# Query split of a cross-attention search: fetching the first tile's columns in the stage and the other seven tiles' during the first tile's search

## The reference

```python
Q = (x_text @ Wq).reshape(Bb, Tt, H, DH)
K = (x_vision @ Wk).reshape(Bb, Gg, H, DH)
scores = jnp.einsum('bthd,bghd->bhtg', Q, K) / np.sqrt(DH).astype(np.float32)
scores = jnp.where(vision_mask[:, None, None, :], scores, -jnp.inf)
topv, topi = jax.lax.top_k(scores, K_TOP)        # K_TOP = 32
probs = jax.nn.softmax(topv, axis=-1)
attn = jnp.zeros_like(scores).at[bi, hi, ti, topi].set(probs)
attn_mean = attn.mean(axis=1)
c_t = jnp.einsum('btg,bgd->btd', attn_mean, x_vision @ Wv) * text_mask[..., None]
```

## Time and profile before

| what | value |
|---|---|
| median of 3 executions | 1713.12 us (1707.66 to 1718.37) |
| the profiled execution, its own time | 1714.1 us |
| its span | 1712.2 us |
| mean granted TensorE clock | 0.921 of full speed |
| busy: TensorE, VectorE, ScalarE, GpSimd | 82%, 75%, 55%, 41% of the span |
| bytes moved by DMA | 37.34 MB |

### The profile page before, as it was taken

The page is one execution under the profiler, slowest core; times in us unless marked ns, Lnnn a source line. Parts: engine busy times, 40 slices in busy tenths (PEclk is TensorE's granted clock), DMA queues, the critical chain, the costliest instruction groups (busy, mean ns, idle before and its releaser), DMA issues. The chain is left out here.

```text
span 1712.2 us, 20081 instructions
## 1 busy us (share of the span) xinstructions
PE 1399.5 (82%) x6652; PEld 718.6 (42%) x6653; DVE 1280.9 (75%) x3087; ACT 943.4 (55%) x1500; POOL 706.9 (41%) x545
## 2 busy tenths in 40 slices
PE   5777799999987657889888898988957539999798
PEld 2223344333334512455454444544645423333365
DVE  4999667855515669999999999999948566766433
ACT  4665211566623302888888888888821236666321
POOL 2664212022002000989998898989810030000012
PEclk9899899999997967999999999999978658999899
DMA  6000111000009420000000000000030120000000
GB/s 148 1 1 0 33 56 42 0 1 0 0 5 201 86 63 1 1 1 1 1 1 1 1 1 1 1 1 1 1 96 9 34 64 1 1 1 1 1 1 13
DMA packets 29962, 37.34 MB, mean 22 GB/s; under 512 B 12975, under 2 KB 23087, under 8 KB 28723
## 3 DMA queue, kind: packets, MB, share of 16 engines
q1 hardware_dynamic: 27294, 22.31, 4.8%
q10 hardware_dynamic: 2552, 13.63, 3.9%
HBM read 29.68 MB, written 6.24 MB: 21 GB/s over the span
## 5 line engine op out<-in xcount | busy, mean ns | idle before, releaser
L1557 PE MATMUL psum<-film_ka,film_context_qa 97*128 97x512 bf16 (+1 forms) x832 | 323.7, 390 | 89.3 <-DVE search_and_weigh_e L1791 38.1
L1758 DVE MAX8 search_and_weigh_kept<-psum 128x8 f32<-128x171 f32 (+2 forms) x1216 | 331.5, 327 | 14.4 <-PE psum L1559 14.1
L1559 PE MATMUL psum<-film_kb,film_context_qb 128*128 128x512 bf16 (+1 forms) x832 | 320.3, 386 | 0.0
L1944 ACT ACTIVATE search_and_weigh_e<-psum,search_and_weigh_bias 128x512 f32<-128x512 f32 (+1 forms) x416 | 268.1, 666 | 60.6 <-PE psum L1559 58.7
L1791 DVE SCALAR_TENSOR_TENSOR search_and_weigh_e<-psum,film_context_top,search_and_weigh_e 128x512 f32<-128x512 f32 (+1 forms) x283 | 200.6, 716 | 14.2 <-ACT search_and_weigh_e L1944 12.4
L1814 POOL TENSOR_TENSOR search_and_weigh_e<-search_and_weigh_e,search_and_weigh_keep 128x512 f32<-128x512 f32 (+1 forms) x133 | 150.6, 1132 | 100.1 <-ACT search_and_weigh_keep L1923 96.8
L1557 PEld LDWEIGHTS psum<-film_ka,film_context_qa 97*128 97x128 bf16 x832 | 86.0, 103 | 237.9 <-DVE search_and_weigh_e L1791 103.3
L3057 POOL TENSOR_TENSOR residual<-residual,top_expert_kept 128x1024 f32<-128x1024 f32 x7 | 16.4, 2348 | 295.4 <-DVE top_expert_kept L3014 295.4
L1818 POOL TENSOR_TENSOR search_and_weigh_mean<-search_and_weigh_e 128x512 f32<-128x512 f32 (+1 forms) x104 | 133.5, 1284 | 11.5 <-DVE search_and_weigh_e L1791 4.3
L1848 PEld LDWEIGHTS psum<-ctx_rows,search_and_weigh_mean_T 128*128 128x128 f32 (+1 forms) x816 | 122.6, 193 | 30.4 <-issue 4.1
L1823 POOL TENSOR_TENSOR search_and_weigh_mean<-search_and_weigh_mean,search_and_weigh_e 128x512 f32<-128x512 f32 (+1 forms) x104 | 128.0, 1230 | 8.2
(11 more groups left out here) (549 smaller groups left out, 2642.6 us busy)
## 6 DMA issues: line engine op xcount, KB each, us to landing
film_kb<-film_k_rows ACTq DMA_DIRECT2D x4, 1601.0 KB
film_ka<-film_k_rows ACTq DMA_DIRECT2D x3, 1601.0 KB
ctx_T<-in_ctx_T SPq DMA_DIRECT2D x1, 2401.5 KB
gqa_experts_w<-in_L_ffn_W SPq DMA_DIRECT2D x1, 2048.0 KB
film_convolve_back<-in_dft_back SPq DMA_DIRECT2D x1, 1728.0 KB, 13.3
film_k_rows<-cross_attention_film_hi SPq DMA_DIRECT2D x6, 256.0 KB, 2.1
film_k_rows<-cross_attention_film_mid SPq DMA_DIRECT2D x6, 256.0 KB, 2.0
film_k_rows<-cross_attention_film_low SPq DMA_DIRECT2D x6, 256.0 KB, 2.0
```

Of the source, the lines that this page charges most:

```text
L1557: pe.matmul(out, a["qa"][0:ROWS, h, rows], a["ka"][0:ROWS, h, c + b:c + b + cols], start=True, stop=False)
L1559: last = pe.matmul(out, a["qb"][:, h, rows], a["kb"][:, h, c + b:c + b + cols], start=False, stop=True)
L1758: last = dve.max(kept[:, h % 2, first + s, :], bank[:, lo:hi])
L1944: act.activation(e[:, n % RING, sub, 0:PIECES[u][1]], ps[:, SEARCH_BANKS + q % WEIGH_BANKS, 0:PIECES[u][1]], ACT.Exp, bias=bias[:, i % 2, ...
```

## The change

The DRAM tensor `q_rows` and a new semaphore `other_tiles` are made in `film_context`, so that both blocks can use them. The helper `fetch_queries` issues the fetches of one part for a given range of columns. In `split_queries`, ScalarE's seven fetches now bring columns 0 to 127 only, that is the first of the eight tiles: 32 KB each instead of 256 KB, still in 128 pieces. SyncE still waits for seven landings. In `search_and_weigh`, SyncE begins with seven fetches of columns 128 to 1023 (224 KB each), ahead of its loads of `mask8` and `w_v`. TensorE waits for `other_tiles` before piece r = 52, the first piece of tile 1. What is computed stays the same.

```diff
--- before.py
+++ after.py
@@ -1453,10 +1453,23 @@
          "eighth": m.sb("eighth", [P, NT * NH]),
          "mask8": m.sb("mask8", [P, NT], U8), "mask": m.sb("mask", [P, NT]), "w_v": m.sb("w_v", [DC, D]),
 
-         "count": m.sb("count", [1, NT * NH + 1], mybir.dt.int32)}
+         "count": m.sb("count", [1, NT * NH + 1], mybir.dt.int32),
+         "q_rows": nc.dram_tensor("q_rows", (3, P, S), BF16).ap(), "other_tiles": m.sem("other_tiles")}
     for part in (split_queries, search_and_weigh, search_general, weigh_again):
         with ExitStack() as ctx:
             part(nc, g, t, Memory(nc, ctx, part.__name__), a)
+
+
+
+QUERY_PLACES = ((("qa", 0), ("qb", 0), ("qb", 2)), (("qa", 1), ("qb", 1), ("qb", 3)), (("qa", 2),))
+N_FETCHES = 7
+
+
+def fetch_queries(eng, a, k, cols, done):
+
+    for name, r in QUERY_PLACES[k]:
+        eng.dma_start(a[name][r * DH:(r + 1) * DH, :, cols],
+                      a["q_rows"][k].rearrange("(h d) s -> d h s", d=DH)[:, :, cols]).then_inc(done, 16)
 
 
 def split_queries(nc, g, t, m, a):
@@ -1473,7 +1486,7 @@
     rest = m.sb("rest", [P, S])
     parts = m.sb("parts", [P, 3, S], BF16)
     hi, mid, low = (parts[:, k, :] for k in range(3))
-    q_rows = nc.dram_tensor("q_rows", (3, P, S), BF16).ap()
+    q_rows = a["q_rows"]
 
     loaded, ones_set, chain_dve = m.sem("loaded"), m.sem("ones_set"), m.sem("chain_dve")
     var_ready, root_ready, xn_ready, xT_psum, xT_ready, q_done, q_ready = (
@@ -1493,7 +1506,7 @@
             sp.dma_start(w_q[:], t["L1_xattn_Wq"]).then_inc(loaded, 16)
             for k in range(3):
                 store(k)
-            sp.wait_ge(spread, 16 * 7)
+            sp.wait_ge(spread, 16 * N_FETCHES)
 
         @block.vector
         def _(dve):
@@ -1530,15 +1543,9 @@
                 act.activation(q[:, n * HALF:(n + 1) * HALF], ps[:, 2 + n, :], ACT.Copy,
                                scale=float(DH) ** -0.5).then_inc(q_ready, 1)
 
-            def fetch(k, places):
+            for k in range(3):
                 act.wait_ge(stored[k], 16)
-                for dst, r in places:
-                    act.dma_start(dst[r * DH:(r + 1) * DH, :, :],
-                                  q_rows[k].rearrange("(h d) s -> d h s", d=DH)).then_inc(spread, 16)
-
-            fetch(0, ((qa, 0), (qb, 0), (qb, 2)))
-            fetch(1, ((qa, 1), (qb, 1), (qb, 3)))
-            fetch(2, ((qa, 2),))
+                fetch_queries(act, a, k, slice(0, P), spread)
 
         @block.gpsimd
         def _(pool):
@@ -1854,6 +1861,8 @@
 
             if search_piece(r):
                 i, h, u = search_piece(r)
+                if r == NH * NCH:
+                    pe.wait_ge(a["other_tiles"], 16 * N_FETCHES)
                 if r >= SEARCH_BANKS:
                     pe.wait_ge(searched, r - SEARCH_BANKS + 1)
                 score_unit(pe, a, ps, r % SEARCH_BANKS, i, h, *PIECES[u]).then_inc(search_done, 1)
@@ -1979,6 +1988,8 @@
         @block.sync
         def _(sp):
             if searching:
+                for k in range(3):
+                    fetch_queries(sp, a, k, slice(P, S), a["other_tiles"])
                 sp.dma_start(mask8[:], t["text_mask"].rearrange("(i p) -> p i", p=P),
                              allow_slow_non_contiguous=True).then_inc(loaded, 16)
                 sp.dma_start(w_v[:], t["L1_xattn_Wv"]).then_inc(loaded, 16)
```

## The result

| | before | after |
|---|---|---|
| median, 20 executions each | 1715.28 us (1707.66 to 1719.41) | 1709.97 us (1703.46 to 1713.33) |
| ratio | 1 | 0.9967, 95% interval 0.9957 to 0.9978 |
| profiled execution: span | 1712.2 us | 1704.6 us |
| mean granted clock | 0.921 | 0.922 |

By the ratio the kernel is 5.7 us faster (0.0033 x 1715), with an interval of 3.8 to 7.4 us; the two medians themselves lie 5.3 us apart. The change is far under 1%, and it stands clear of the scatter only because 20 executions of each were taken: the interval leaves 1 out.

A forecast was written before the change was run, and what follows sets the result against it. VectorE bounds the search, whose start waits for the query split's last fetch landing. Gaining 6.2 us there, with the other three parts at 0, takes the median from 1713.1 to 1707 us, range 1702 to 1713.

The forecast's parts named there:

- Part 1: Query split stage: with 256 B pieces ScalarE's issuing sets the pace, last landing 2.0 us; 6.2 us gained (4.3 to 6.5).
- Part 2: Search block: SyncE's fetches of the other seven tiles are hidden by VectorE's 47 us on tile 0; cost 0.
- seven fetches in 3 to 3.5 us: Profile sign at the start of the search: SyncE issues its seven fetches in 3 to 3.5 us.
- The price of the cover: Search start: cost if the other tiles' transfers were all exposed instead of hidden by tile 0's search, 9.4 us.
- Part 3: Start of the search: about 9 us of transfers beside it do not slow it; cost 0.
- Part 4: Start of the search: TensorE begins at 1.2 GHz before and after, the 1.2 us loss unchanged; cost 0, about 1 us either way.
- A: Query split stage: a fetch costs by pieces, not bytes, so nothing is gained; time 1713, chance 0.04.
- C: Start of the search: code loads wait behind the fetches, 3 us of stall, half the gain lost; time 1710, chance 0.06.
- B: 1260 to 1440 us: TensorE's clock falls from 0.72 and gives the gain back; at 0.66 time 1716 to 1717; chance 0.10.

The follow-up runs named there:

- traffic later: Against the changed kernel, SyncE issues the other tiles' fetches only after two heads of the first tile are searched; 1706.6 us, one execution.
- fetched twice: Against the changed kernel, SyncE fetches the other tiles' columns twice and TensorE waits for both before the 53rd piece; 1710.7 us, one execution.

## Why the prediction was right

**The sum.** Forecast: 6.2 us less, 1707, range 1702 to 1713. Measured: 1709.97 us, 5.7 us less by the ratio (3.8 to 7.4), and 6.4 and 6.0 us in two more sets; the gap itself is 6.4 us shorter. The median of before was itself 2.2 us higher with 20 executions than with 3, which accounts for most of the distance between 1707 and 1710.

**Part 1, the short fetches.** Right in mechanism and size. A piece of 256 B was put between 10 and 27 ns and took 16; the landing of the last fetch was put at 2.0 us and took 1.8 to 1.9, as 610.7 - 608.67 against 611.6 - 609.72; the wait was to fall to 4.7 and fell to 4.5 us. The step that carried the forecast was the comparison of 8.75 us of data with 3.3 us of issuing: it said that ScalarE would set the pace, so that not 7/8 of the 8.2 us, 7.2, but 6.2 are won. The series of one, two, four and eight tiles has that crossing, between two and four. The Trainium skill's rule on pieces under 512 B (DMA: Bandwidth & Descriptors, Specifications) was read in the prediction as twice the bytes, which would make a 256 B piece cost about what one of 512 B does. It cost 16 ns against 26, so by the byte 1.2 times as much and not twice.

**Part 2, the cover.** Right. No wait at the 53rd piece, 47 us behind the first (46.6 measured), and the loads of mask and w_v came to their end at 616.46 + 7.3 = 623.8 us (forecast 624). That agreement is in part luck: the last of the seven fetches landed at 615.51 + 7.3 = 622.8 us, where 620.5 was forecast, and w_v only 1.0 us behind it. The sign "seven fetches in 3 to 3.5 us" missed as well: they took 3.95, since one of the seven took over 1 us. The price of the cover was sized too low: 9.4 us forecast, 10.4 to 10.5 measured when it stood open. The issues are not the term at fault: where none was slow and the seven took 3.2 us, the last still landed 10.2 us behind the first issue. What the sum had too small is the time around the data: it put the last landing 1.7 us above 7/8 of the old 8.75 us (9.4 - 7.7), of which 0.4 us were the start and 1.3 us had no row. Measured are 2.5 to 2.8 us. The data themselves were sized right: the queue of SyncE took 0.560 x 15 = 8.4 us of the 16 engines in 611 to 626 us of the kernel after, and without the 0.7 us of mask and w_v (11.7 / 16) that is 7.7. It cost nothing, with some 35 us to spare.

**Part 3, traffic beside the search.** Right, 0 us, now with the traffic doubled and with it taken away.

**Part 4, the clock at the start.** Right: 1.2 GHz for the first 5 us in both kernels, VectorE busy for 3.83 and 3.85 us of them.

**The rivals.** A fell by the series of tiles, C by the doubled traffic. B, a clock that gives the whole gain back in 1260 to 1440 us, is ruled out by the times, which are 5.7 to 6.4 us shorter. Its sign in the profile is there in part: in 180 us that begin 17.4 us before the convolution stage, as 1260 to 1440 us do before, the mean clock is 0.72 and 0.73 in the two profiles of before and 0.68 to 0.71 in the twelve others (0.70 in the first of after, which by the prediction's own working would cost 3 us). So the place was well chosen, and whether a part of B is real stays open, as said above. The stage is also why single profiles mislead. The first pair gave 7.6 us (1712.2 - 1704.6) although the stage took 2.9 us more after, so 4.1 us came from elsewhere in the kernel; a second pair gave -5.2 (1709.3 - 1714.5), with 7.9 us more in the stage.

## What to carry to other kernels

When a load at the end of a stage holds a barrier, ask which part of it the next stage touches first, and how long it works on that part: here an eighth of the bytes was needed at once, the rest 47 us later. What is won is not the share of the bytes but the distance to the next link, here the seven DMA issues on one engine, so a further cut of the bytes (two tiles or one) is worth 0.2 us, while an earlier store is worth 2 us of the stage. Where single executions scatter by more than the effect, measure the effect between two instructions of the stage itself, and show with an idle pause that the end follows it.

## What the runs showed of the hardware that was not expected

- A memset of 3.51 us on GpSimd (1 x 4096 bf16) stretched a VectorE cast from 0.42 to 1.26 us, and after it was moved, a tensor_scalar of 8 columns from 0.17 to 1.14 us; both ended 0.02 to 0.28 us behind the memset.
- A packet of the seven fetches took 16, 26, 60 and 139 ns with pieces of 256, 512, 1024 and 2048 B: twice the bytes cost 1.6 times as much at first and then 2.3 times, more than their share. Why is open.
- In all eleven profiles in which SyncE issues seven fetches at the start of the search's block, one of them took 0.89 to 1.47 us instead of 0.43. In the two bursts that came later (traffic later, and the second one of fetched twice) none did. What delays it at the block's start is open; where the transfers stood open, it cost some 0.3 us.
